# The layer norms' reciprocal square roots in two steps on two engines: Sqrt on ScalarE, reciprocal on VectorE

## The reference

```python
x = x + _L0_conv_ref(_gn(x), ...)   # mixture of experts on 2x2 patches
x = x + _L1_conv_ref(_gn(x), ...)   # deformable 3x3 convolution, batch norm, relu
x = x + _L2_conv_ref(_gn(x), ...)   # S4D filter, gated unit, layer norm over 256, decoder
x = x + _L3_conv_ref(_gn(x), ...)   # 7x7 depthwise, layer norm over 32, MLP
```

```python
mu = jnp.mean(x, axis=-1, keepdims=True)
var = jnp.var(x, axis=-1, keepdims=True)
return (x - mu) * jax.lax.rsqrt(var + eps) * gamma + beta
```

## Time and profile before

| | us |
|---|---|
| median of 3 runs | 1703.65 |
| lowest and highest of them | 1702.98, 1705.48 |
| profiled execution, its own time | 1701.32 |
| its span in the trace | 1699.4 |

### The profile page before, as it was taken

How to read it: one execution, slowest core, us unless ns; L and a number is a source line. 1 busy time by engine, 2 the same in 40 slices (tenths; PEclk the granted TensorE clock), 3 DMA queues, 4 the chain that set the end, 5 groups by cost and what they waited for, 6 DMA issues and landing times.

```text
span 1699.4 us, 14008 instructions
## 1 busy us (share of the span) xinstructions
PE 1340.9 (79%) x4202; PEld 611.5 (36%) x4202; DVE 982.0 (58%) x1645; ACT 547.2 (32%) x874; POOL 1217.9 (72%) x1418
## 2 busy tenths in 40 slices
PE   6968953999959958879979848779749654798797
PEld 5743321444424313324434213334314221343345
DVE  2455553535663479853754588934532694445785
ACT  1222211323342331243533312243413304244445
POOL 8677777756777777777777777777777777777700
PEclk9988976999989978979989969989969876899899
DMA  6322323421332222321332222322221112322000
GB/s 214 79 76 77 83 70 85 120 77 53 83 87 75 65 58 76 94 75 51 92 95 59 64 58 80 96 69 70 61 78 52 49 54 58 82 64 68 24 10 16
DMA packets 111882, 123.08 MB, mean 72 GB/s; under 512 B 50880, under 2 KB 88896, under 8 KB 111424
## 3 DMA queue, kind: packets, MB, share of 16 engines
q0 software_dynamic: 36864, 75.57, 15.9%
q1 hardware_dynamic: 73888, 43.14, 9.9%
q10 hardware_dynamic: 1056, 3.47, 0.6%
HBM read 99.79 MB, written 9.01 MB: 64 GB/s over the span
## 4 chain that ended last, share of the span: by engine, by line
POOL 32%; PE 31%; DVE 16%; issue 12%; ACT 5%; DMA 2%; SPq 1%; ACTq 0%; DVEq 0%; POOLq 0%
POOL gt L1132 32%; PE bank L1954 6%; PE bank L1967 5%; DVE rb L1726 5%; PE bank L1868 4%; PE bank L1860 3%; PE bank L1878 3%; PE bank L1904 3%; DVE gt L1610 2%; PE bank L1937 1%; DVE he L1508 1%; DVE gt L1612 1%; PE bank L2011 1%; PE bank L1976 1%; DVE bst L1433 1%
## 5 line engine op out<-in xcount | busy, mean ns | idle before, releaser
L1132 POOL DMA_INDIRECT gt<-corner_table,idx x1152 | 1145.6, 994 | 378.0 <-issue 347.5
L1954 PE MATMUL bank<-u,wk 128*128 128x512 f32 x512 | 241.8, 616 | 7.0 <-DMA u<-sqb 7.0
L1610 DVE TENSOR_TENSOR gt<-gt,bank 128x1152 f32<-128x1152 f32 x128 | 172.6, 1348 | 112.5 <-DMA gt<-corner_table,idx 111.6
L1967 PE MATMUL bank<-yg,wts 128*128 128x512 f32 x512 | 235.3, 604 | 0.4 <-DVE rb L1666 0.2
L1868 PE MATMUL bank<-xg,w_sb 128*128 128x512 f32 (+1 forms) x288 | 147.6, 596 | 47.1 <-DVE xg L1499 25.0
L1924 PE MATMUL bank<-cst,sm 128*128 128x128 f32 x384 | 75.5, 312 | 116.6 <-DVE sm L1618 116.4
L1726 DVE SCALAR_TENSOR_TENSOR rb<-xp,par,rb 128x1024 f32<-128x1024 f32 x124 | 154.9, 1290 | 0.0
L1205 ACT ACTIVATE he<-bank 128x512 f32<-128x512 f32 (+1 forms) x144 | 79.0, 549 | 228.2 <-PE bank L1860 227.8
L1508 DVE SCALAR_TENSOR_TENSOR he<-he,bank 128x512 f32<-128x512 f32 (+1 forms) x144 | 89.7, 625 | 106.7 <-PE bank L1868 103.6
L1652 DVE SCALAR_TENSOR_TENSOR tg<-tg,ae 128x512 f32<-128x512 f32 x64 | 44.1, 691 | 182.1 <-ACT ae L1303 182.0
L1860 PE MATMUL bank<-xp,w_sb 128*128 128x512 f32 (+1 forms) x288 | 142.0, 576 | 4.5 <-ACT he L1205 4.5
(11 more groups left out here) (249 smaller groups left out, 1469.7 us busy)
## 6 DMA issues: line engine op xcount, KB each, us to landing
gt<-corner_table,idx POOLq DMA_INDIRECT x1152
tb<-gate_of_token SPq DMA_DIRECT2D x56, 256.0 KB, 5.0
u<-sqb SPq DMA_DIRECT2D x48, 128.0 KB, 2.7
corner_table<-tb SPq DMA_DIRECT2D x36, 128.0 KB, 2.6
w_sb<-w ACTq DMA_DIRECT2D x2, 1024.0 KB, 6.8
xp<-xg SPq DMA_DIRECT2D x56, 32.0 KB
X<-x SPq DMA_DIRECT2D x1, 1536.0 KB, 11.0
out<-X SPq DMA_DIRECT2D x6, 256.0 KB, 2.2
```

What stands on the lines that cost most here:

```text
L1132: pool.indirect_dma_start(gt[:, t % GRING, k].rearrange("p a c -> p (a c)"), None, corners, bass.IndirectOffsetOnAxis(ap=idx[s % 2][:, j, ...
L1610: ch.then(tt(rows, rows, share.unsqueeze(2).to_broadcast([P, 4 * KK, C]), ALU.mult))
L1954: op = mm(psum[b][:, :], wk[:, t, d], u4[:, g, at:at + HALF], start=t == 0, stop=t == JJ - 1 and n > 0)
L1967: op = mm(psum[B2.bank(*name)][:, :], w_glu[:, k, col + d * P:col + (d + 1) * P], yg[:, c % 2, k], start=k == 0, stop=k == NB2 - 1)
```

## The change

In layer 2's end, ScalarE takes Sqrt of `var2` in place and signals `std2_ready`; VectorE waits for it, takes the reciprocal of `var2` in place and waits for its own result. In layer 3, ScalarE takes Sqrt of every half; VectorE waits for the half, takes its reciprocal, and when the reciprocals of all halves are done it multiplies. The Exp instructions and two semaphores are gone.

```diff
@@ l2_end, ScalarE
-                act.activation(var2[r, :], var2[r, :], ACT.Ln, bias=epst[r, :]).then_inc(S["ln2_ready"], 1)
-                act.wait_ge(S["ln2_ready"], closed(s, q) + 1)
-                act.activation(var2[r, :], var2[r, :], ACT.Exp, scale=-0.5).then_inc(S["rstd2_ready"], 1)
+                act.activation(var2[r, :], var2[r, :], ACT.Sqrt, bias=epst[r, :]).then_inc(S["std2_ready"], 1)
@@ l3_center, ScalarE
-                    act.activation(ysq_(s, n), psum[b][:, 0:width(s)], ACT.Ln, bias=epst[:, :]).then_inc(free[b], 1)
-                for n in halves(s):
-                    B2.read(act, "sq3", s, n)
-                    act.activation(ysq_(s, n), ysq_(s, n), ACT.Exp, scale=-0.5).then_inc(S["rstd3_ready"], 1)
+                    act.activation(ysq_(s, n), psum[b][:, 0:width(s)], ACT.Sqrt, bias=epst[:, :]).then_inc(free[b], 1)
@@ l2_end, VectorE
-                dve.wait_ge(S["rstd2_ready"], closed(s, q) + 1)
+                dve.wait_ge(S["std2_ready"], closed(s, q) + 1)
+                ch.then(dve.reciprocal(var2[both(s, q), :], var2[both(s, q), :]))
@@ l3_scale, VectorE
                 for n in halves(s):
-                    dve.wait_ge(S["rstd3_ready"], nth(s, n) + 1)
+                    B2.read(dve, "sq3", s, n)
+                    ch.did(dve.reciprocal(ysq_(s, n), ysq_(s, n)))
+                ch.wait()
+                for n in halves(s):
                     B2.read(dve, "mu3", s, n)
                     tt(yc_(s, n), yc_(s, n), ysq_(s, n), ALU.mult).then_inc(S["yz_ready"], 1)
```

## The result

| | before | after |
|---|---|---|
| median us (6 runs each, same chip) | 1703.73 | 1712.95 |
| lowest and highest | 1702.54, 1705.48 | 1709.66, 1715.90 |
| profiled execution, its own time | 1701.32 | 1713.94 |
| its span | 1699.4 | 1712.0 |

The changed kernel takes 1.0053 of the time of before, with a 95% interval of 1.0039 to 1.0067: 9.2 us or 0.54% slower. The sign was forecast, and the time lies in the range. The size was not: 6.1 us were forecast.

What follows compares the result with a forecast made beforehand. GpSimd was taken to bound the body, and a VectorE, ScalarE and TensorE chain the tail; 0 (body) + 1.15 + 2.2 - 0.1 (tail) + 2.9 (clock) = 6.1 us on 1703.65 gave 1709.8 us, range 1703 to 1717.

Steps and rivals of the forecast that it cites:

- The bound, and the two questions: GpSimd bounds 413 to 1589 us, then a 110 us chain; is the body's cover thick enough, what does the tail pay?.
- The price of a wide reciprocal: VectorE's reciprocal of 512 columns, extrapolated from one and eight columns: 3.0 us, perhaps 3.4; 256 columns 1.6 us.
- The rival with 4.5 us: Reciprocal half as dear again, GpSimd's cover tears at tile 116 and loses 3.9 us; 15.3 us slower, 1719; chance 0.14.
- In all: Whole kernel: 18 reciprocals add 51 us to VectorE; 21 table loads and 18 Exps take 38 us from ScalarE.
- First end: Layer 2 end at 1595 us, behind the last gather: reciprocal and handovers 3.1 us instead of 1.96, so +1.15 us.
- Middle stretch: Tail from 1650 to 1669 us: two reciprocals, partly behind taps, against removed loads and Exps; L1681 starts 2.2 us later.
- Narrow scales: Two 256-column scales in the tail: no cost at 1675 us, -0.1 us at the last.
- The clock: TensorE's two tail idle stretches grow to 4.0 and 5.6 us; half speed behind them costs 1.4 and 1.5, together 2.9 us.
- The body: Ahead of the last gather, 13 reciprocals cost 0: the cover at tiles 107 and 116 holds by 0.6 us each.
- The last gather within 1 us of 1588.7.: Sign in the changed profile that GpSimd's body is unharmed; a move of more than 2 us would prove the forecast wrong.
- The sum: Whole kernel: body 0, tail 1.15 + 2.2 - 0.1, clock 2.9, making 6.1 us slower, 1709.8 us.

Runs made afterwards that it cites:

- tail_only: Kernel before with the new Sqrt and reciprocal form only in the two layer 2 ends and three folded scales behind the last gather; ratio 1.0042.
- keep_more: Changed kernel with TensorE's two long idle stretches behind the last gather filled by matmuls nobody reads; ratio 1.0030 to the kernel before.
- before_again: The kernel before, unchanged, run and profiled once more; 1708.31 us in its single run, 113.2 us from the last gather to the end.
- tail_ends: Kernel before with the new form only in the two layer 2 ends behind the last gather; ratio 1.0031.

## Why the prediction was right, and where it missed

**The bound, and the two questions.** Right. GpSimd still paces the body, and the tail pays in full: tail_only has four fifths of the loss.

**The price of a wide reciprocal.** 3.0 us was taken, 3.35 measured ("it could be 3.4" was the better half of that sentence). The failed step is the extrapolation: seven columns more between two rows of 164 and 203 ns give the slope only to a tenth or so, and 512 columns multiply the error. The measurement decides. The rival with 4.5 us fell, and with it its 15 us. Its mechanism did not: the prediction let the cover tear from about 3.2 us a reciprocal on, and at 3.35 it tore.

**In all.** VectorE 57 us more (forecast 51, all of the difference the reciprocal's price), ScalarE 37 less (38).

**First end.** Forecast +1.15, measured +1.57. 0.33 of the difference is the step from ScalarE's function to the product (1.48 us longer, not 1.15), which is the reciprocal's price; the other 0.1 was not followed up.

**Middle stretch.** Forecast +2.2, measured +2.84. Its parts: Sqrt's end to the first product 3.42 us instead of 1.97 (+1.45, forecast +1.12); from there to the second function -0.61 (forecast -0.13 and the load, -0.57 together); from the second function's end to the product 3.97 instead of 1.97 (+2.00, forecast +1.63). Right in kind, and short by 0.35 us for each of the two reciprocals.

**Narrow scales.** Forecast -0.1, measured +0.06 at the last:

```profile
1700.58 0.47 ACT L1344 ACTIVATE gt<-bank,epst 128x256 f32<-128x256 f32 x1
1701.09 1.75 DVE L1751 RECIPROCAL gt<-gt 128x256 f32<-128x256 f32 x1 [2.27 <-ACT gt L1344]
1702.88 0.43 DVE L1755 TENSOR_TENSOR gt<-gt 128x256 f32<-128x256 f32 x1
```

1700.58 + 0.47 to 1702.88 is 1.83 us, against 1.77 in the earlier trace rows.

**The clock.** Both idle stretches came out as worked out (4.25 for 4.0, 5.54 for 5.6), and half clock stands behind both. The first cost 1.63 us (forecast 1.4), the second 0.40 in this profile and 1.92 in the next (forecast 1.5). What the prediction had wrong is the baseline: it took the clock of before as full at both places, since its profile showed that, and with the same 2.2 us of idle time it fell in three and in two of five profiles. Of 2.9 us forecast about 1.6 belong to the change. keep_more gave back 4 us in time and 2.2 in its trace; the intervals cover the difference, and nothing more is known of it.

**The body.** This is the step that failed. Forecast 0, with 0.6 us left at tiles 107 and 116; measured about 1.6 us, with two tears. Tile 107 held (1.8 us left in all five profiles with the new body, against 2.8 on the mean with the old one). At tile 116 the delay was 4.8 us on the mean, not 3.95: the reciprocals of the end and the scale were each 0.35 us dearer, 1.05 in all, close to that difference. The prediction did say "with 3.4 us a reciprocal the excess at tile 116 is some 0.6 us", and it was 1.2. Tile 64 was not among its places. Before, it had 8.1 us left, and now 1.1, which is the least it needs. VectorE was 3.5 us later than before behind the first end (its sample started at 502.78 instead of 499.27), but 2.1 of these it had brought along from ahead of the end; the end added 1.4. Where TensorE's half clock lasted longer, some 1.4 more came on top (eight state matmuls took 6.65 us instead of 5.30). How the rest up to 7 us gathered on the way to tile 64 was not followed. In two of the five profiles with the new body the tile did not wait: it had 1.9 us left in one and 6.9 in the other. And the cover itself differed from profile to profile (3.0 to 6.3 us at tile 116 with the same text), so that 0.6 us of margin in one profile could not carry a zero.

**"The last gather within 1 us of 1588.7."** Wrong as a test. By the prediction's own words a move of more than 2 us spoke against it, and the move was 6.0. But with the old body and no new wait it came between 1587.1 and 1593.5 us, in six profiles; with the new one between 1591.3 and 1596.6, in five. So the 6.0 us between the two first profiles are 1.9 us of waits and otherwise mostly this spread: 1.7 us of them were there at 368 us, ahead of the first changed instruction.

**The sum.** Forecast 0 + 1.15 + 2.2 - 0.1 + 2.9 = 6.1. Measured by the runs: about 1.6 (body), 4.4 (chain of the tail), 1.6 (clock): 7.6 us, against 9.2 [6.6, 11.4] in time. The clock's term was 1.3 us too large and the body's and the chain's together some 2.8 too small; that the sum is not further off is in part luck. The 1.6 us between lie within the intervals, and no run assigned them. One place where they may lie was not tested. On the mean of the profiles the last gather came 3.5 us later with the new body, and only 1.2 of these are waits; the gathers' own durations added 2.0 (1149.5 us against 1147.5). With a spread of 7.3 us between profiles of the old body, it stays open whether the change slows the gathers down.

## What to carry to other kernels

To move work from an engine with time to spare to another is worth what stands between the two engines at the end of each chain, not what either saves in busy time: here a table load of 1.28 us and an Exp of 0.63 us made room for a reciprocal of 3.35 us, at each of the nine layer 2 ends. A wide operation that the trace holds only in narrow forms needs its own measurement, since its price multiplies into every term. And a margin (of cover, of clock) that is thinner than its own spread between two executions is to be counted at its chance, not at zero: look at the same place in a second profile of the unchanged kernel before leaning on it.

## What the runs showed of the hardware

- Reciprocal on VectorE takes about 6.25 ns for each fp32 column and 0.15 us besides, with 64 and with 128 partitions alike: 3.35 us for 512 columns, against 0.69 for a product of the same shape.
- With about 2.2 us of idle time ahead of the same matmuls TensorE's clock sometimes fell to half and sometimes stayed (5 of 10 cases). Up to 1.6 us of idle time it never fell (6 cases), from 3.8 us on it always did (12 cases). Matmuls that nobody reads, put into the idle time, kept it full. Where it fell against the idle time differed: with the first matmuls behind it in before_again (1.00 from 1605.8 to 1608.0, 0.52 from 1608.0 to 1611.5), but still within it in tail_ends, whose matmuls start at 1608.10. TensorE by stretch, tail_ends:

```profile
1603.20:1606.40 3.20, 0.00 (x0) 1.00 0.00 0
1606.60:1608.00 1.40, 0.00 (x0) 0.50 0.00 0
```

- In the six profiles with the old body the 1152 gathers took 1142.8 to 1150.1 us in all (the page of each run). That spread of 7.3 us is more than any wait of the body that this change made.
